# A two-expert-layer attention kernel: routing arithmetic of the second layer partly on GpSimd, its tables in three pieces, its first tile inside the attention's last step

## The chip, the cores and the metric

The kernel runs on one core of a Trainium2 chip. The time is the device time of one launch in microseconds; for the kernel before, the median of three runs is given. Engines are called as the profile calls them: PE (TensorE), DVE (VectorE), ACT (ScalarE), POOL (GpSimd), SP (SyncE, which here only issues DMAs).

## The reference

```python
x = x + 0.5 * ffn(layernorm(x))      # top-1 of 8 experts, 128 -> 512 -> 128
x = x + attn(layernorm(x))           # 16 sequences of 256 tokens, 16 heads of 8
x = x + 0.5 * ffn(layernorm(x))      # the same experts again

def ffn(x, Wr, br, W1, b1, W2, b2):
    expert = argmax(x @ Wr.T + br, axis=-1)
    h = relu(einsum('td,efd->etf', x, W1) + b1[:, None, :])
    y = einsum('etf,edf->etd', h, W2) + b2[:, None, :]
    return y[expert, arange(tokens)]
```

x is 16 x 256 x 128 in fp32, that is 4096 rows, or 32 tiles of 128 rows. The attention has rotary embeddings and a normalisation of q and k by head.

## The kernel before, in words

**Three stages.** The first expert layer (`experts(0)`), the attention (64 steps of one head group of one sequence, `step(n)`, n from 0 to 63 and a few more that drain it) and the second expert layer (`experts(1)`). An expert layer sorts the rows by expert into 39 tiles of 128 slots (`S_TILES`; each tile holds rows of one expert). For tile t, `x_transpose(t)`, `up(t)` (L862) and `down(t)` (L878) run on PE, `scale`, `load`, half of `relu` and `output` on DVE, the other half of `relu` and the copy of the expert's weights into `Ws` (`w_copy`) on ACT.

**What each step n of the attention does.** ACT takes exponentials of 2 x 512 columns (`exps`, L1231), PE makes the scores (L981), the products with the values (L1005) and, six steps ahead, scores for the row maxima (L958), which DVE reduces (L1769, `maxima`). For each sequence DVE multiplies the rotated q and k by their inverse roots (Rn, L1752), and POOL splits Rn into parts (`split`, L705 and L712). Each engine has its own list of instructions, written by its own `step(n)`; tables at the head of the file (`..._AT`) say at which n a piece of other work stands in it.

**The routing of the second layer** goes on under the attention, in four lots of tiles, `ROUTE_LOTS` = 0 to 11, 12 to 19, 20 to 25, 26 to 31. For a lot: mean and variance (`lot_layernorm` on POOL or `layernorm` on DVE), the inverse deviation (ACT, L1140 and L1142), logits (`lot_logits`), the one-hot choice (`one_hot`, `pick`), a running count over the lot's tiles (`lot_seen`: 8 scans, one for each expert), the count over partitions (`rank` on PE, L825 to L827), read back by `lot_take`, the slot of each row (`lot_place`: two tensor ops, a reduction and a cast on DVE), and at last one indirect DMA a tile from POOL that writes 128 rows into the DRAM tensor `slots` (`place`, L623). Behind each such DMA POOL writes 352 columns of a tile that nobody reads (`pause`, L603). Lots 0 to 2 are done in the attention, lot 3 within the tiles of the second layer (`last_lot(t, place)` spreads its DVE work over tiles 7 to 13).

**The tables.** `full_table` works out from the counts of the first three lots which expert and which rows of `slots` the first 19 tiles (`FULL`) have. SP waits for it and for all stores of lots 0 to 2, and then fetches tile after tile from `slots` (L536). `last_lot` makes the table of the other 20 tiles. There is a ring of 15 buffers for fetched tiles (`R_X2`): tile t + 15 is fetched when tile t has been written out.

**The end.** POOL's loop over t issues `scatter(t)`, an indirect DMA that writes tile t's rows to `out` (L632) as soon as DVE's `output` has finished them, with a pause of 480 columns behind. Before t = 3 stands the norm of lot 3, before t = 4 its logits, and behind t = 8 (`STORES_BEHIND`) the six stores of lot 3.

```python
for t in range(S_TILES):
    if t == LAST["norm"]:
        lot_layernorm(N_LOT + 1 + LAST_LOT)
    if t == LAST["logits"]:
        lot_logits(LAST_LOT)
    scatter(t)
    if t == STORES_BEHIND:
        for j in range(*ROUTE_LOTS[LAST_LOT]):
            place(LAST_LOT, j)
```

`fill_const` issues matmuls whose result nobody reads: 5 in step 50 (`FILL_TURN`), 6 in step 58, 9 behind the last step of the attention (`FILL_END`).

Of the kernel before, what the change touches and what calls it, by code (L numbers as in the profile page):

```python
# [5 lines left out]
P = 128  # L6
# [37 lines left out]
for RAMP_X in (RAMP_PE, RAMP_ACT, RAMP_DVE):  # L44
# [20 lines left out]
POOL_NORM_AT = {32: 0, 45: 1}  # L65
POOL_LOGITS_AT = {35: 0, 48: 1}
NORM_AT = {56: 2}
INVERSE_AT = {34: 0, 47: 1, 57: 2}
LOGITS_AT = {57: 2}
HOT_AT = {37: 0, 49: 1, 57: 2}  # L70
PICK_AT = {38: 0, 50: 1, 57: 2}
SEEN_AT = {38: 0, 50: 1, 57: 2}
RANK_AT = {41: 0, 53: 1, 59: 2}
PLACE_AT = {42: 0, 54: 1, 59: 2}
STORE_AT = {43 + j: (j,) for j in range(12)} | {55: (12, 13), 56: (14, 15), 57: (16,), 58: (17, 18), 59: (19,),
                                                60: (20, 21), 61: (22, 23), 62: (24, 25)}
TABLE_AT = 60
# [5 lines left out]
STORES_BEHIND = 8  # L83
LATE_LOADS = 3
DRAIN_FIRST = {1: (65,)}
DRAIN_SECOND = {2: (66, 67), 3: (68,)}
# [7 lines left out]
def program(nc, x, wqkvT, wpT, g_rms, wrT, br, w1T, b1, w2T, b2,  # L94
# [14 lines left out]
    with ctx:  # L109
# [52 lines left out]
        Hot, Seen = (e_major[:].rearrange("p e j -> p j e") for e_major in (HotE, SeenE))  # L162
# [24 lines left out]
        Done = sb("Done", [P, N_EXP + 1])  # L187
        Run = sb("Run", [P, len(ROUTE_LOTS), N_EXP], BF16)
# [87 lines left out]
        lot_ready = sem("lot_ready")  # L276
        lg_terms = sem("lg_terms")
# [63 lines left out]
        END = N_ALL + 5  # L341
        LOT = [None, slice(0, 2), slice(2, CH)] + [slice(CH * c, CH * c + CH) for c in range(1, N_CHUNK)]
# [123 lines left out]
        def _(sp):  # L466
# [83 lines left out]
            sp.wait_ge(offs_ready, 2)  # L550
# [12 lines left out]
        def _(pool):  # L563
# [1454 lines left out]
```

## Time and profile before

| | |
|---|---|
| median of 3 runs | 482.1 us (481.16 to 483.43) |
| the profiled execution | 479.99 us |
| its span | 478.2 us |
| PE busy | 427.5 us (89%) |
| DVE busy | 382.0 us (80%) |
| ACT busy | 349.1 us (73%) |
| POOL busy | 349.1 us (73%) |
| granted TensorE clock, mean | 0.99 |

The span runs from the first to the last instruction; the time of the execution is 1.8 us longer. Busy shares are means over stages that have different limits, so the stage in question has to be looked at by itself. A timeline row has the start in us from the start of the span, the busy time in us, engine, line and operation, out<-in, the count of merged instructions, and in brackets how long the engine had been idle before and who ended that.

### The profile page before, as it was taken

To read this page: it belongs to the slowest core of one execution; us is meant where nothing else is said; L and a number is where in the kernel's file an instruction comes from. 1 tells how busy PE (TensorE), PEld (TensorE's weight loads), DVE (VectorE), ACT (ScalarE), POOL (GpSimd) and SP (SyncE) were. 2 spreads that over 40 slices of the span, in tenths; PEclk is the share of its full clock that TensorE was granted. 3 is DMA by queue.
4 is the path that set the end of the run, shared out by engine and by line. 5 is a ranking of instruction groups with operands and counts; after the bars stand their busy time and mean duration, and the time that the engine had idled before them with its cause. 6 is when DMAs were issued, how large, how long until landed. Compare 5 with 4: busy or idle time off the path is not lost.

```text
span 478.2 us, 14075 instructions
## 1 busy us (share of the span) xinstructions
PE 427.5 (89%) x4140; PEld 318.0 (66%) x4140; DVE 382.0 (80%) x1055; ACT 349.1 (73%) x782; POOL 349.1 (73%) x561
## 2 busy tenths in 40 slices
PE   7999999989878898999989998998888979899993
PEld 4347999767764565665656665565455559789993
DVE  4786788897888788988889889988888557687772
ACT  4416776777747998989989898888677947467771
POOL 8019898978857988698683974399766807798995
PEclk9899999999999999999999999999999999899998
DMA  7872434251100000000000000000011123223310
GB/s 205 252 290 57 95 86 152 64 178 42 29 25 18 14 15 14 13 8 14 10 14 2 3 3 3 2 13 14 21 36 37 36 54 80 74 71 96 77 33 13
DMA packets 28651, 27.03 MB, mean 57 GB/s; under 512 B 5685, under 2 KB 25948, under 8 KB 28019
## 3 DMA queue, kind: packets, MB, share of 16 engines
q1 hardware_dynamic: 24034, 17.65, 12.4%
q0 software_dynamic: 4544, 8.49, 6.6%
q8 instruction: 37, 0.61, 0.5%
q14 instruction: 36, 0.29, 0.2%
HBM read 16.56 MB, written 12.71 MB: 61 GB/s over the span
## 4 chain that ended last, share of the span: by engine, by line
PE 41%; DVE 23%; issue 12%; POOL 12%; ACT 7%; DMA 2%; DVEq 1%; ACTq 0%; POOLq 0%
DVE Smax L1769 8%; PE PS L862 8%; PE PS L878 8%; PE PS L1005 5%; PE PS L958 5%; PE PS L981 4%; POOL out L632 3%; PE PS L940 3%; POOL Unread L603 2%; DVE St L1388 2%; DMA Pt<-rows,TokI 2%; ACT Pt L1231 2%; PE PS L924 2%; PE PS L917 1%; PE PS L1035 1%
## 5 line engine op out<-in xcount | busy, mean ns | idle before, releaser
L1769 DVE TENSOR_REDUCE Smax<-PS 128x4 f32<-128x1024 f32 x128 | 155.8, 1224 | 30.8 <-PE PS L958 30.0
L1231 ACT ACTIVATE Pt<-PS 128x1024 f32<-128x1024 f32 x128 | 126.4, 1024 | 18.4 <-PE PS L981 15.1
L878 PE MATMUL PS<-W,HsT 128*128 x624 | 85.2, 280 | 3.7 <-DVE Ys L1640 3.6
L862 PE MATMUL PS<-XsT,Ws 128*128 128x128 f32 x624 | 84.0, 278 | 1.0 <-ACT XsT L1135 0.7
L878 PEld LDWEIGHTS PS<-W,HsT 128*128 128x128 f32 x624 | 76.8, 194 | 6.7 <-issue 5.7
L862 PEld LDWEIGHTS PS<-XsT,Ws 128*128 128x128 f32 x624 | 77.3, 194 | 4.5 <-ACT XsT L1135 1.9
L1005 PE MATMUL PS<-Pt,Vg 128*32 128x256 f32 x1024 | 68.5, 385 | 0.4
L705 POOL TENSOR_TENSOR HL<-Rn,Zero 128x512 fp32r<-128x512 f32 x28 | 35.3, 1283 | 38.1 <-DVE Rn L1752 36.6
L610 POOL DMA_INDIRECT Pt<-rows,TokI x39 | 40.3, 1034 | 29.9 <-DVE TokI L1586 19.4
L603 POOL MEMSET Unread<- 128x352 f32 (+1 forms) x140 | 62.0, 443 | 0.2
L958 PE MATMUL PS<-QkT 24*128 24x256 f32 x512 | 59.7, 306 | 2.0 <-DVE Smax L1769 1.7
L958 PEld LDWEIGHTS PS<-QkT 24*128 24x128 f32 x512 | 39.9, 184 | 28.1 <-ACT Pt L1231 22.8
L1629 DVE TENSOR_SCALAR HsT<-PS,Bs 128x128 f32<-128x128 f32 x144 | 43.8, 347 | 18.1 <-PE PS L862 17.0
L1135 ACT ACTIVATE Ws<-W 128x512 f32 x78 | 49.0, 631 | 10.9 <-DVE ExpI L1593 6.7
L1176 ACT ACTIVATE HsT<-PS,Bs 128x128 f32<-128x128 f32 x168 | 51.6, 367 | 5.1 <-PE PS L862 4.4
L632 POOL DMA_INDIRECT out<-AtCol x39 | 38.4, 985 | 20.7 <-DVE AtCol L1640 15.2
L1135 ACT ACTIVATE XsT<-PS 128x128 f32<-128x128 f32 x78 | 21.7, 279 | 43.2 <-PE PS L851 42.4
L981 PE MATMUL PS<-QkT 25*128 25x256 f32 x512 | 34.2, 325 | 18.7 <-DVE Smax L1769 9.9
L1135 ACT ACTIVATE QkT<-PS 128x512 fp32r<-128x512 f32 x64 | 38.4, 600 | 15.3 <-PE PS L940 14.4
L940 PE MATMUL PS<-I,HL 128*128 128x128 f32 x256 | 41.5, 285 | 6.0 <-DVE Smax L1769 3.6
L981 PEld LDWEIGHTS PS<-QkT 25*128 25x128 f32 x512 | 22.1, 183 | 33.2 <-issue 31.2
L623 POOL DMA_INDIRECT slots<-XX,SlotI x32 | 31.6, 986 | 14.5 <-ACT Pt L1231 10.0
(255 smaller groups left out, 725.2 us busy)
## 6 DMA issues: line engine op xcount, KB each, us to landing
AtCol<-slots SPq DMA_DIRECT2D x39, 65.5 KB, 1.9
rows<-XX SPq DMA_DIRECT2D x8, 288.0 KB, 4.3
XX<-x SPq DMA_DIRECT2D x8, 256.0 KB, 4.2
W<-w1T SPq DMA_DIRECT2D x2, 1024.0 KB, 6.2
W<-w2T SPq DMA_DIRECT2D x2, 1024.0 KB, 9.1
mid<-mid_second SPq DMA_DIRECT2D x1, 1472.0 KB
mid<-Ys SPq DMA_DIRECT2D x16, 64.0 KB
QkT<-NmaxT SPq DMA_DIRECT2D x64, 4.0 KB
```

The source lines that it names most:

```text
L603: nc.gpsimd.memset(Unread[:, 0:columns], 0.0).then_inc(paused, 1)
L632: pool.indirect_dma_start(out, bass.IndirectOffsetOnAxis(ap=Xs2[:, t % R_X2, P + 2:P + 3].bitcast(I32), axis=0), Xs2[:, t % R_X2, 0:P], No ...
L862: last = nc.tensor.matmul(PS[:, h_bank(n) + c // 2, (c % 2) * P:(c % 2 + 1) * P], Ws[:, n % R_WS, c * P:(c + 1) * P], XsT[:, n % 2, :], st ...
L878: last = nc.tensor.matmul(PS[:, y_bank(n), 0:P], HsT[:, n % 2, c, :], W2[:, ds(e * D_FF + c * P, P)], start=(c == 0), stop=(c == FC - 1))
L940: last = nc.tensor.transpose(PS[:, qkT_bank(m), qk * T + tt * P:qk * T + (tt + 1) * P], v, I[:])
L958: last = nc.tensor.matmul(PS[:, max_bank(m, pair) + h % 2, tt * T:(tt + 1) * T], QkT[rows, m % R_QK, 0, tt * P:(tt + 1) * P], QkT[rows, m ...
L981: last = nc.tensor.matmul(PS[:, score_bank(m, h // 2) + h % 2, c * T:(c + 1) * T], QkT[rows, m % R_QK, 1, c * P:(c + 1) * P], QkT[rows, m ...
L1005: last = nc.tensor.matmul(PS[32 * h:32 * h + 32, 6, 0:T], weights[:, c, at:at + 32], Pt[:, m % 2, h, c, :], start=(m % 2 == 0 and c == 0), ...
L1135: return nc.scalar.activation(dst, src, ACT.Copy)
L1176: last = nc.scalar.activation(HsT[:, n % 2, c, :], PS[:, h_bank(n) + c // 2, (c % 2) * P:(c % 2 + 1) * P], ACT.Relu, bias=Bs[:, n % 2, c:c ...
L1231: nc.scalar.activation(Pt[:, m % 2, 2 * pair:2 * pair + 2, :, :].rearrange("p h c t -> p (h c t)"), PS[:, score_bank(m, pair):score_bank(m ...
L1769: nc.vector.tensor_reduce(Smax[:, b % 2, :, at:at + 33:32].rearrange("p t h -> p h t"), PS[:, max_bank(m, pair):max_bank(m, pair) + 2, :]. ...
```

## The change

Lot work moves between engines and between steps:

- DVE's 8 scans a lot become one scan over all experts (`seen`, with a mask `FreshLot` of ones and zeros); the one-hot choice of a lot is cut into `lot_largest`, `lot_ties` and `lot_pick` in different steps.
- The slot arithmetic (`lot_place`) leaves DVE. POOL's new `lot_slots` does it in six dependent instructions.
- Norm and logits of lot 2 go from DVE to POOL.
- The stores of lots 0 to 2 stand later (`STORE_AT`: from step 48 to 64, where it was 43 to 62); for lot 2 the `rank` on PE moves from step 59 to 61.
- The expert table is made in three pieces: 13 tiles (`FIRST_FULL`) from lots 0 and 1, six more from lot 2 (`more_tiles`, `more_table`), 20 with lot 3. SP fetches the first 13 tiles when lots 0 and 1 are stored.
- The second layer begins in PE's step 64 (`begin`, `first`): tile 0 is transposed and multiplied before the last product with the values. DVE's `begin` stands in step 62; POOL copies the first three tiles' expert weights in step 60 (`first_weights`).
- The 5 filling matmuls of step 50 and the 9 at the end are gone, as is the `drain` of POOL between its attention steps and its loop over t.
- In that loop, norm and logits of lot 3 stand before t = 0, and `lot_slots` and the stores of lot 3 behind t = 4. DVE starts on lot 3 at t = 6 instead of 7.

```diff
-POOL_NORM_AT = {32: 0, 45: 1}
-POOL_LOGITS_AT = {35: 0, 48: 1}
-NORM_AT = {56: 2}
-RANK_AT = {41: 0, 53: 1, 59: 2}
+POOL_NORM_AT = {32: 0, 44: 1, 57: 2}
+POOL_LOGITS_AT = {35: 0, 46: 1, 59: 2}
+LARGEST_AT = {38: 0, 50: 1, 59: 2}
+SEEN_AT = {46: 0, 54: 1, 60: 2}
+RANK_AT = {47: 0, 55: 1, 61: 2}
+POOL_SLOT_AT = {47: 0, 55: 1, 61: 2}
+WEIGHTS_AT = 60
+TABLE_AT, SCALE_AT, MORE_AT = 58, 62, 63
-STORES_BEHIND = 8
+STORES_BEHIND = 4
-FILL_TURN, FILL_MAXIMA, FILL_END = {50: 5}, {58: 6}, 9
-LAST = {"norm": 3, "inverse": 6, "logits": 4, "rank": 9}
+FILL_MAXIMA = {58: 6}
+LAST = {"norm": 0, "inverse": 5, "rank": 9}
...
+            def over_experts(into, values, r, op):
+
+                lot_link(nc.gpsimd.tensor_tensor(Half[:, r], values[:, r, 0:4], values[:, r, 4:8], op))
+                lot_link(nc.gpsimd.tensor_tensor(Half[:, r, 0:2], Half[:, r, 0:2], Half[:, r, 2:4], op))
+                lot_link(nc.gpsimd.tensor_tensor(into[:, r], Half[:, r, 0], Half[:, r, 1], op))
+
+            def lot_slots(i):
+                r = LOT_ROWS[i]
+                shape = [P, r.stop - r.start, N_EXP]
+                pool.wait_ge(*emptied("rank", i))
+                lot_link(nc.gpsimd.tensor_tensor(Place[:, r], by_tile(SeenE, r), Base[:].unsqueeze(1).to_broadcast(shape), ALU.add))
+                lot_link(nc.gpsimd.tensor_tensor(Place[:, r], Place[:, r], by_tile(HotE, r), ALU.mult))
+                over_experts(SlotF, Place, r, ALU.add)
+                nc.gpsimd.tensor_copy(SlotI[:, r], SlotF[:, r]).then_inc(lot_ready, 1)
+
+            def first_weights():
+                pool.wait_ge(slots_ready, 2)
+                for t in range(R_WS):
+                    e = pool.value_load(tile_expert(1, t), min_val=0, max_val=N_EXP - 1)
+                    nc.gpsimd.tensor_copy(Ws[:, (S_TILES + t) % R_WS, :], W1[:, ds(e * D_FF, D_FF)]).then_inc(ws_ready, 1)
...
-            nc.gpsimd.drain()
             for t in range(S_TILES):
                 if t == LAST["norm"]:
                     lot_layernorm(N_LOT + 1 + LAST_LOT)
-                if t == LAST["logits"]:
                     lot_logits(LAST_LOT)
                 scatter(t)
                 if t == STORES_BEHIND:
+                    lot_slots(LAST_LOT)
                     for j in range(*ROUTE_LOTS[LAST_LOT]):
                         place(LAST_LOT, j)
...
+                if n == TAIL - 1:
+                    pe.wait_ge(exp_ready, 2 * n - 1)
+                    begin()
                 if n < 0 or not group(n + QKT_LEAD):
                     small(n)
+                if n == TAIL - 1:
+                    first()
...
-                for e in range(N_EXP):
-                    last = nc.vector.tensor_tensor_scan(Seen[:, r, e], OneCol[:, r], Hot[:, r, e], 0.0, ALU.mult, ALU.add)
-                return last
+                return nc.vector.tensor_tensor_scan(flat(SeenE, r), FreshLot[:, N_EXP * r.start:N_EXP * r.stop], flat(HotE, r), 0.0, ALU.mult, ALU.add)
...
+            def lot_largest(i):
+                r = LOT_ROWS[i]
+                dve.wait_ge(lg_ready, i + 1)
+                mark(nc.vector.tensor_reduce(Mx[:, r], Lg[:, r], AX, ALU.max))
+                settled()
+                mark(tt_(by_tile(HotE, r), Lg[:, r], over_experts(Mx, r), ALU.is_ge))
```

**The order on POOL, steps 55 to 61, after the change.** The engine that stores the rows; the six rows with Place, Half and SlotF are `lot_slots` of lot 1, those with Dm, Mean and Var the norm of lot 2, those with XX and Lg its logits, and "COPY Ws" a weight copy.

```order
L772 CAST SlotI<-SlotF 128x8
L647 DMA slots<-XX,SlotI 33920x131
L627 MEMSET Unread 128x352
L647 DMA slots<-XX,SlotI 33920x131
L627 MEMSET Unread 128x352
L647 DMA slots<-XX,SlotI 33920x131
L627 MEMSET Unread 128x352
L682 TENSOR_TENSOR Dm<-St 128x6
```

Three stores (tiles 11 to 13) stand between the slots of lot 1 and the norm of lot 2. The same engine, from the norm's last instruction to the logits of lot 2:

```order
L692 TENSOR_TENSOR Var<-Var,Dm 128x6
L647 DMA slots<-XX,SlotI 33920x131
L627 MEMSET Unread 128x352
L647 DMA slots<-XX,SlotI 33920x131
L627 MEMSET Unread 128x352
L647 DMA slots<-XX,SlotI 33920x131
L627 MEMSET Unread 128x352
L647 DMA slots<-XX,SlotI 33920x131
L627 MEMSET Unread 128x352
L744 TENSOR_TENSOR XX<-Mean,XX 128x6
L746 TENSOR_TENSOR Lg<-Lg,XX 128x48
```

Four more stores (tiles 14 to 17) stand between that norm and the logits. Before, POOL had nothing but stores at this place; the slots of lot 1 and the norm and logits of lot 2 were DVE's.

**The order on PE, steps 60 to 65.** L1005 and L1065 are products with the values, L981 and L1041 scores, L825 to L827 and L881 to L883 the rank of lot 2, L862 and L918 `up`. As it was, from step 59:

```order
L825 MATMUL PS<-Run,Ones 128x8
L826 MATMUL PS<-SeenE,Ahead 128x8
L827 MATMUL PS<-Run,Ones 128x8
L1025 MATMUL PS<-I,Yn 128x128 x2
L1005 MATMUL PS<-Pt,Vg 32x256 x8
L981 MATMUL PS<-QkT 128x256 x8
L1035 MATMUL PS<-Wp,YnT 128x136 x2
L1005 MATMUL PS<-Pt,Vg 32x256 x8
L981 MATMUL PS<-QkT 128x256 x8
L1015 MATMUL PS<-I,YuT 128x128 x4
```

The rank stood ahead of the turn of Yn (L1025). The same engine as it is now, from step 60:

```order
L1095 MATMUL PS<-Wp,YnT 128x136 x2
L1065 MATMUL PS<-Pt,Vg 32x256 x8
L1041 MATMUL PS<-QkT 128x256 x8
L881 MATMUL PS<-Run,Ones 128x8
L882 MATMUL PS<-SeenE,Ahead 128x8
L883 MATMUL PS<-Run,Ones 128x8
L1075 MATMUL PS<-I,YuT 128x128 x4
L1065 MATMUL PS<-Pt,Vg 32x256 x8
L1041 MATMUL PS<-QkT 128x256 x8
```

The rank, which waits for DVE's count of lot 2, stands two steps later, right before the turn of the last but one sequence's outputs (L1015, now L1075).

**The order on POOL at the head of the second layer, after the change** (L656 is `scatter`):

```order
L744 TENSOR_TENSOR XX<-Mean,XX 128x6
L746 TENSOR_TENSOR Lg<-Lg,XX 128x48
L748 TENSOR_SCALAR XX<-XX 128x6
L749 TENSOR_TENSOR Lg<-Lg,Br 128x48
L656 DMA out<-AtCol 4096x128
L627 MEMSET Unread 128x480
L656 DMA out<-AtCol 4096x128
```

Before, three scatters stood ahead of the norm and one more ahead of the logits; now norm and logits stand ahead of all 39.

## Rows read from the trace of the kernel before

**Rows 1.** Timeline of POOL, from lot 3's stores to the end.

```profile
415.69 0.97 POOL L623 DMA_INDIRECT slots<-XX,SlotI  x1 [0.83 <-DVE SlotI L1913]
...
471.98 0.97 POOL L632 DMA_INDIRECT out<-AtCol  x1 [0.16 <-issue]
473.26 0.97 POOL L632 DMA_INDIRECT out<-AtCol  x1 [0.30 <-issue]
```

**Rows 2.** Timeline of all engines, from the attention's last exponential to tile 0.

```profile
381.16 1.02 ACT L1231 ACTIVATE Pt<-PS 128x1024 f32<-128x1024 f32 x1
381.26 0.97 POOL L623 DMA_INDIRECT slots<-XX,SlotI  x1 [0.17 <-issue]
...
385.42 13.88 SPq L536 DMA_DIRECT2D AtCol<-slots  x14
...
388.33 1.16 PE L862 MATMUL PS<-XsT,Ws 128*128 128x128 f32 x8 [0.37 <-ACT XsT L1135]
```

**Rows 3.** Timeline of PE, up(5), and the rank of lot 3.

```profile
399.24 1.06 PE L862 MATMUL PS<-XsT,Ws 128*128 128x128 f32 x8
...
410.14 0.17 PE L825 MATMUL PS<-Run,Ones 128*128 128x8 bf16 x1 [2.15 <-DVE Run L1895]
```

**Rows 4.** Busy time by stretch: us, PE, PEld, DVE, ACT, POOL, clock, DMA share, GB/s.

```profile
383.50:388.30 4.80, 2.36 (x12) 0.87 (x10) 0.78 (x4) 0.79 (x3) 0.00 (x0) 1.00 0.17 43
...
408.00:414.40 6.40, 4.26 (x24) 4.14 (x25) 3.83 (x27) 1.61 (x6) 4.72 (x8) 0.73 0.19 56
```

**Rows 5.** Timeline of POOL, steps 51 and 52: the split of sequence 15, stores.

```profile
341.31 2.52 POOL L705 TENSOR_TENSOR HL<-Rn,Zero 128x512 fp32r<-128x512 f32 x2 [1.85 <-DVE Rn L1752]
...
345.49 0.99 POOL L623 DMA_INDIRECT slots<-XX,SlotI  x1 [0.16 <-issue]
...
347.06 0.97 POOL L623 DMA_INDIRECT slots<-XX,SlotI  x1 [0.17 <-issue]
```

**Rows 6.** Timeline of DVE, step 50: lot 1's choice, scans, and Rn.

```profile
336.00 0.22 DVE L1429 TENSOR_REDUCE Mx<-Lg 128x8 f32<-128x64 f32 x1 [0.66 <-POOL Lg L725]
...
339.68 0.71 DVE L1443 TENSOR_TENSOR_SCAN SeenE<-OneCol,HotE 128x8 bf16<-128x8 f32 x8
...
340.54 0.69 DVE L1752 TENSOR_TENSOR Rn<-Rot,Rr 128x512 f32<-128x512 f32 x1
```

**Rows 7.** Timeline of POOL: norm of lot 1 (first, last), logits of lot 3.

```profile
321.63 0.22 POOL L658 TENSOR_TENSOR Dm<-St 128x8 f32<-128x8 f32 x1
...
323.32 0.20 POOL L668 TENSOR_TENSOR Var<-Var,Dm 128x8 f32<-128x8 f32 x1
...
404.27 0.28 POOL L722 TENSOR_TENSOR Lg<-Lg,XX 128x48 f32<-128x48 f32 x1
...
405.36 1.04 POOL L632 DMA_INDIRECT out<-AtCol  x1 [0.23 <-issue]
```

**Rows 8.** Timeline of DVE, steps 58 to 60: lot 2, a residual, the table.

```profile
367.97 0.20 DVE L1422 TENSOR_TENSOR Lg<-Lg,XX 128x48 f32<-128x48 f32 x1
...
370.48 0.17 DVE L1503 TENSOR_TENSOR Run<-Run,SeenE 128x8 bf16<-128x8 bf16 x1
...
373.92 0.42 DVE L1790 TENSOR_TENSOR XX<-PS,XX 128x256 f32<-128x256 f32 x1 [1.50 <-PE PS L1035]
...
379.28 0.16 DVE L1531 TENSOR_TENSOR Done<-End 128x7 f32<-128x7 f32 x1
```

**Rows 9.** Timeline of PE and of ACT: rank of lot 2, exponentials of steps 60 and 62.

```profile
370.80 0.17 PE L825 MATMUL PS<-Run,Ones 128*128 128x8 bf16 x1 [0.31 <-DVE Run L1503]
...
373.02 1.94 ACT L1231 ACTIVATE Pt<-PS 128x1024 f32<-128x1024 f32 x2 [0.35 <-PE PS L981]
...
377.59 1.94 ACT L1231 ACTIVATE Pt<-PS 128x1024 f32<-128x1024 f32 x2 [0.29 <-PE PS L981]
```

**Rows 10.** Timeline of ACT: the half of relu(5), the inverse of lot 3.

```profile
400.62 0.62 ACT L1176 ACTIVATE HsT<-PS,Bs 128x128 f32<-128x128 f32 x2
...
403.26 0.21 ACT L1142 ACTIVATE XX<-LnVar 128x6 f32<-128x6 f32 x1
```

More of the change, by code:

```diff
@@ L825, in rank @@
                     nc.tensor.matmul(PS[:, bank, 0:N_EXP], Ones[:], Run[:, i - 1, :], start=True, stop=False)
-                last = nc.tensor.matmul(PS[:, bank, 0:N_EXP], Ahead[:], Seen[:, ROUTE_LOTS[i][1] - 1, :], start=(i == 0), stop=True)
+                last = nc.tensor.matmul(PS[:, bank, 0:N_EXP], Ahead[:], lot_total(i), start=(i == 0), stop=True)
                 last = nc.tensor.matmul(PS[:, bank, N_EXP:2 * N_EXP], Ones[:], Run[:, i, :], start=True, stop=True)
@@ new lines, in begin, with first, run @@
+                def begin():
+                    pe.wait_ge(slots_ready, k + 1)
+                    x_transpose(0)
+                def first():
+                    up(0)
+                    x_transpose(1)
+                def run():
+                    for t in range(1 if k else 0, S_TILES + 1):
+                        if k and t - 1 in TABLES:
+                            pe.wait_ge(slots_ready, TABLES[t - 1])
+                        if t < S_TILES:
+                            up(t)
+                        if t >= 1:
+                            e = pe.value_load(tile_expert(k, t - 1), min_val=0, max_val=N_EXP - 1)
+                        if k and t == LAST["rank"]:
+                            rank(LAST_LOT)
+                        if not k and tail(t):
+                            max_scores(t - TAIL_TILE, 0)
+                        if k:
+                            for n in DRAIN.get(t, ()):
+                                step(n)
+                        if t + 1 < S_TILES:
+                            x_transpose(t + 1)
+                        if t >= 1:
+                            down(t - 1, e)
+                        if not k:
+                            if t == WP_TURN:
+                                wp_turn()
+                            if t == WP_ROUTER:
+                                wp_router()
+                            for n in RAMP_PE.get(t, ()):
+                                step(n)
@@ L915, in fill_const @@
+                return begin, first, run
             def fill_const(count, bank=7):
@@ L1195, in run @@
                     for t in range(S_TILES):
-                        if k:
-                            for n in DRAIN_FIRST.get(t, ()):
-                                step(n)
-                        first = not tail(K0 + t) and not (k and t in DRAIN_SECOND)
+                        first = not tail(K0 + t) and not (k and t in DRAIN)
                         if first and t + 1 < S_TILES:
@@ L1367, in _ @@
             begin, run = experts(1)
-            for n in range(RAMP_END, TAIL):
+            for n in range(RAMP_END, TAIL - 1):
                 step(n)
-                if n == TAIL - 2:
-                    begin()
             run()
@@ L1423, in scaled_logits, with ranks, over_experts, settled @@
                 link(tt_(Lg[:, r], Lg[:, r], Br[:].unsqueeze(1).to_broadcast(shape), ALU.add))
+            def ranks(r):
+                return Rank[:].unsqueeze(1).to_broadcast([P, r.stop - r.start, N_EXP])
+            def over_experts(values, r):
+                return values[:, r].unsqueeze(2).to_broadcast([P, r.stop - r.start, N_EXP])
+            def settled():
+                dve.wait_ge(step_done, links[0])
+            def mark(ins):
+                links[0] += 1
+                ins.then_inc(step_done, 1)
@@ L1688, in rope_tables @@
                 half = HD // 2
+                link(nc.vector.memset(FreshLot[:], 1.0))
+                for r in LOT_ROWS:
+                    nc.vector.memset(FreshLot[:, N_EXP * r.start:N_EXP * r.stop:r.stop - r.start], 0.0)
                 dve.wait_ge(rope_in, 16 * 5)
```

434 lines of the change are left out of this document (222 added, 212 removed).

## Prediction

> **What bounds the kernel now.** I read the end first. POOL's timeline shows that the last 36 indirect DMAs (six stores of lot 3, then the scatters of tiles 9 to 38) follow each other without a real gap: from 415.69 to the 35th at 471.98 are 34 times 1.655 us, and the last comes 1.28 us later, at 473.26, since it has no pause ahead [rows 1]. Where a wait would stand, "issue" stands with 0.16 to 0.30 us. So the end is set by POOL's queue; the span of 478.2 us ends 4.9 us behind the start of the last scatter. PE runs at 1.9 us a tile there, slower than POOL empties its queue, but POOL began late.
>
> Then the joint of attention and second layer. The last exponential ends at 382.18, POOL's last store of lot 2 starts at 381.26, SP sees it landed and fetches the first tiles at 385.42, and up(0) starts at 388.33 [rows 2]. A store is thus visible 4.2 us behind its start, and 2.9 us more pass until the first tile is on PE. up(5) is at 399.24, and before up(10) PE idles 2.15 us for the rank of lot 3 [rows 3]; in the stretch around that wait the granted clock is 0.73, so about half of it ran at 1.2 GHz [rows 4].
>
> **The change, by the path that sets the end.** A faster PE in the second layer buys nothing by itself; what counts is when POOL can start its unbroken queue. Now norm and logits of lot 3 stand ahead of scatter(0), and the logits wait for ACT's inverse behind relu(5). Call T0 the start of scatter(0). All 45 indirect DMAs and the new slot arithmetic follow it. So I work out T0 and then add the queue.
>
> *1. Split of sequence 15.* From here on POOL will be full. It starts at 341.31 now, when DVE has made Rn [rows 5]. In step 50 DVE spends 0.66 us waiting for POOL's logits, about 0.9 on the first three ops and 1.4 on pick and eight scans (0.71) before Rn at 340.54 [rows 6]. The change leaves there two ops of about 0.25 each, so 2.4 us of DVE's time go; part was cover for the maxima's matmuls, and I count 1.9. From lot 0, seven scans and the slot arithmetic (1.2 us) leave DVE, spread over steps 38 to 43; about half of DVE's time there showed up in the steps, so 0.9. The split starts at 338.5. Bounds: 341.3 (nothing gained) and 337.6.
>
> *2. POOL's queue in the attention.* Split to first store 4.2 us, then 1.57 us from this store to the next [rows 5]. Behind the split now come 16 stores (tiles 2 to 17, at 1.55: 24.8), lot_slots(1), the norm of lot 2 and its logits. The norm took 1.9 us (321.63 to 323.52) and with its joint 2.1; the logits with their four instructions 1.2 [rows 7]. lot_slots is six dependent instructions on POOL, which no row shows; its nearest are POOL's small tensor ops, 0.20 to 0.28 us and a hand-over of 0.08: 2.1 us with the joint to the next DMA. Bounds 1.7 and 3.0. Sum 24.8 + 4.2 + 2.1 + 2.1 + 1.2 = 34.4, and the logits of lot 2 are ready at 338.5 + 34.4 = **372.9**. Before, DVE had multiplied them at 367.97 [rows 8].
> On 48 columns the multiplication of the logits takes POOL 0.28 us [rows 7] and DVE 0.20 [rows 8], a ratio of 1.4. The Trainium skill, "GPSIMD Engine Reference", section "Performance versus the Vector engine", puts ordinary elementwise work at about 2x (1.96 for its add) and so speaks against this move; the trace disagrees at this size. By the page's ratio, lot_slots would be an estimated 2.6 us instead of 2.1, and the end 1.0 us later (two lots on the path). I take the rows'.
>
> *3. DVE and PE, steps 59 to 61.* The 13-tile table (4.3 us, from there to 379.44 [rows 8]) stands in step 58 and is done at about 369, ahead of the logits: free. From 372.9 follow choice, scan and running count of lot 2 (367.97 to 370.65 are 2.7 us; less 0.4 for two logits ops and 0.5 for seven scans: 1.8), between them the residual with its statistics (1.0, from 373.92 to the table), then PE's rank: 372.9 + 2.8 + 0.2 = **375.9**. It was at 370.80 and two steps earlier [rows 9]. The exponentials of step 62 need rank, turn, values and scores behind it: 370.80 to 373.02 for the same kind of list, 2.5 with the longer turn. So they start at 378.4, not 377.59 [rows 9]: the attention ends at 382.18 + 0.8 = 383.0 although its steps 38 to 57 were some 3 us faster. All that is saved before is lost in this wait.
> *The clock.* PE reaches the rank at about 370.2 and waits 5.7 us. A wait of 2.15 us brought the granted clock of a stretch to 0.73 [rows 3, 4]: 6.4 us with 27% missing, which is 3.4 us at half speed, 1.7 us of work. I take 1.5 us here; bounds 0 and 3.0. The attention ends at 384.5.
>
> *4. Tile 0.* up(0) follows at once, with 0.4 us for the copy of the transposed tile: **384.9**, 3.4 us earlier than 388.33. The data are there: store 19 starts at 372.9 + 0.2 + 1.6 = 374.7, landed 4.2 later, on PE 2.9 later at 381.8 [rows 2]. POOL's three weight copies are ready by 381 and cost nothing on this path.
>
> *5. up(0) to T0.* up(0) to up(5) takes 10.9 us now; values(63) comes in between (1.0), and DVE's eight small table ops in tiles 1 to 5 (some 1.6 us busy, a third of it felt, 0.5): 12.4. From up(5) to the end of relu(5) on ACT 2.0; inverse 0.5; logits 1.1; joint 0.3 [rows 3, 7, 10]: 3.9. T0 = 384.9 + 16.3 = **401.2**. POOL itself is free by then: two stores, three copies (1 to 1.7 us each), slots, six stores and the norm end near 395.
>
> *6. The queue.* 44 x 1.655 to the last scatter, less 0.37 for the missing pause, plus lot_slots(3) 2.2: 74.6. Last scatter at 475.8, against 473.26 [rows 1]. **+2.5 us.** The rank of lot 3 is no stall any more (its scan is done at t = 7), about 4 us on PE, but PE is not what ends last. For the same reason the later fetches may wait (tile 19 for lot 3's stores, tile 20 for the ring) without cost: PE would end near 471. The drain before the loop cost nothing: POOL had its stores out and no tile to scatter yet. The five and nine filling matmuls lay in waits; their removal is in items 1 and 4, and a clock that falls without them is in the bound of the clock.
>
> The profiled execution took 479.99 us, so the sum gives 482.5; that execution was 2.1 us below the median shown, and I add the difference to the median: 482.1 + 2.5 = **484.6 us**.
>
> **The rivals.** 0.5% is 2.4 us, about what a measurement of this kernel tells from no change. My sum lies at that edge.
> - *A, POOL's queue makes PE wait at step 61 and the clock falls* (forecast): 483.5 to 488, mostly just above +2.4 us. For it: the count of stores between slots(1) and the logits, which is in the order, not a guess. Chance 0.55; of it 0.40 over the edge.
> - *B, the same wait, but no loss of clock, or a shorter queue*: item 3 without the clock gives +1.0, 483.1 us; with lot_slots at its low bound (two lots) 482.3. For it: at the joint before, PE was busy 2.36 of 4.8 us and the clock stayed at 1.00 [rows 4]. Against: the wait now is as long by itself and nothing fills it. Chance 0.22, nearly all within the edge.
> - *C, faster.* If the logits of lot 2 came in time (split at 337.6, DVE slack in steps 51 to 57 used up by nothing), the attention would end at 382.2 - 0.9 - 1.9 - 1.2 (norm of lot 2 off DVE ahead of the last maxima) = 378.2. Then tile 0's data decide. It would need POOL's logits by 369.0, 4 us earlier than I find; store 19 starts then at 370.8, up(0) at 378.6 at best, T0 at 394.9 and the last scatter at 469.5: -3.8, 478.3 us. It decides if POOL's queue from the split takes under 31 us instead of 34.4. Against: 24.8 of them are counted DMAs. Chance 0.18.
> - *D, the second layer starves PE so long that POOL runs dry*, by the late landing of lot 3's stores and half clock: tile 19 on PE at T0 + 18.7 + 4.2 + 2.9 = T0 + 25.8, 20 more tiles 37.9, plus 3 for their waits and 3.5 for the clock, 70.2: still 4 us under the queue's 74.6. At twice those waits and that clock the end would be some 3 us later than A, 487.5. Chance 0.05.
>
> **How the numbers follow.** Forecast 484.6. Slower by over 0.5%: 0.40 from A, 0.05 from D. Within: 0.15 from A, 0.20 from B, 0.01 from C, so 0.36. Faster: 0.17 from C and 0.02 from B, 0.19. The range: below it reaches into C (479.0), above it takes in the clock's high bound, slots at 3.0 and a split that gains nothing, not all at once: 488.0.
>
> **What would show it.** In the profile after: the split at 338 to 339 and POOL unbroken from there to its copies; DVE's Mx of lot 2 released by POOL's Lg near 373; PE idle 5 to 6 us ahead of L881, with a granted clock below 1 behind; up(0) near 385; scatter(0) near 401, released by POOL's own logits, and then 1.65 us a DMA to the end. I am wrong if PE does not wait at the rank of lot 2, if scatter(0) starts before 398, or if the last scatters are released by DVE (then PE sets the end).

## The result and the profile after

The changed kernel takes 485.66 us (median of 17 runs, 483.99 to 487.09), the kernel before 481.44 us beside it (median of 17, 479.71 to 484.75). The ratio is 1.0081 with a 95% interval of 1.0061 to 1.0101: slower by about 4 us. The profiled execution took 485.71 us with a span of 483.9 us. The one of before took 479.99 us with a span of 478.2 us and lay 1.45 us below its median here; so the two profiles differ by 5.7 us where the medians differ by 4.2.

The forecast was 484.6 us, by +2.5 us in POOL's queue of scatters. The time came out 1.1 us from it, but what makes it up is something else, so that the number is close is luck.

First the end of POOL's timeline in the changed kernel, which answers to [rows 1]; columns as there (start, us, engine, line, operation, idle time ahead and what released it).

```profile
461.09 0.97 POOL L656 DMA_INDIRECT out<-AtCol  x1 [0.17 <-issue]
462.06 0.52 POOL L627 MEMSET Unread<- 128x480 f32 x1
462.74 0.97 POOL L656 DMA_INDIRECT out<-AtCol  x1 [0.17 <-issue]
...
473.96 0.97 POOL L656 DMA_INDIRECT out<-AtCol  x1 [0.31 <-issue]
```

The scatters follow each other in 1.65 us without a gap, as before, and the last starts at 473.96, only 0.7 us later than before (473.26). But the span does not end 4.9 us behind that start any more: it ends 9.9 us behind it. What fills this stretch is not in the timeline at all. It is in the list of the instructions that close the program, by engine (count, duration in ns as smallest/median/largest, first and last start in us). In the kernel before it reads:

```profile
L109 ACTq DRAIN  x1: 654/654/654, 468.9 to 468.9; - x1
...
L109 DVEq DRAIN  x1: 330/330/330, 470.9 to 470.9; - x1
L109 POOLq DRAIN  x1: 6164/6164/6164, 471.8 to 471.8; - x1
```

And in the changed kernel:

```profile
L111 ACTq DRAIN  x1: 654/654/654, 462.0 to 462.0; - x1
...
L111 DVEq DRAIN  x1: 330/330/330, 464.0 to 464.0; - x1
L111 POOLq DRAIN  x1: 11391/11391/11391, 472.3 to 472.3; - x1
...
L111 SPq DRAIN  x1: 7/7/7, 476.3 to 476.3; - x1
```

The program closes with a drain on each engine, an instruction that in every trace here ends behind all work of its engine ahead of it. POOL's begins, in the records, while its last work is still under way, so its duration is not its price. From the end of the last scatter (473.96 + 0.97 = 474.94) to the end of the drain (472.3 + 11.39 = 483.68) it is 8.74 us. Before it was 3.74 us (474.23 to 477.97). That is 5.0 of the 5.7 us. The other 0.7 are POOL's queue.

The joint of attention and second layer, first on POOL and then on PE, answers to [rows 2, 5, 8, 9]:

```profile
338.25 2.53 POOL L729 TENSOR_TENSOR HL<-Rn,Zero 128x512 fp32r<-128x512 f32 x2 [1.45 <-DVE Rn L1878]
...
372.44 0.28 POOL L749 TENSOR_TENSOR Lg<-Lg,Br 128x48 f32<-128x48 f32 x1
...
374.58 0.97 POOL L647 DMA_INDIRECT slots<-XX,SlotI  x1 [0.17 <-issue]
...
394.54 0.20 POOL L682 TENSOR_TENSOR Dm<-St 128x6 f32<-128x6 f32 x1 [5.11 <-DVE St L1452]
...
398.60 1.07 POOL L656 DMA_INDIRECT out<-AtCol  x1 [0.25 <-issue]
```

```profile
375.50 0.17 PE L881 MATMUL PS<-Run,Ones 128*128 128x8 bf16 x1 [4.40 <-DVE Run L1579]
...
383.61 1.16 PE L918 MATMUL PS<-XsT,Ws 128*128 128x128 f32 x8
```

The split of sequence 15 starts at 338.25, POOL then has its unbroken list, the logits of lot 2 come at 372.7, and PE waits 4.40 us ahead of the rank. At 394.54 POOL has idled 5.11 us for DVE's statistics of lot 3. The granted clock behind that wait, from the table by stretches (length, busy us and count of PE, PEld, DVE, ACT, POOL, then the clock as a share of 2.4 GHz, DMA share, GB/s):

```profile
370.00:374.00 4.00, 1.10 (x22) 0.44 (x12) 1.04 (x6) 2.59 (x4) 3.52 (x9) 1.00 0.10 34
374.00:378.00 4.00, 2.50 (x23) 1.16 (x23) 2.40 (x11) 0.00 (x0) 3.75 (x8) 0.74 0.12 38
378.00:382.00 4.00, 3.58 (x42) 1.90 (x42) 0.99 (x4) 2.94 (x4) 2.66 (x8) 0.83 0.24 65
```

A quarter and a sixth of the clock are missing in two stretches of 4 us: together 3.4 us at 1.2 GHz. Still PE does its last matmul at 463.97, where it was 470.90 before. PE has become 7 us earlier, and nothing of it reaches the end.

### The profile page after: what moved, and what is told of

Read it like the earlier page. It is cut to its first block, busy times and chain, and to the rows that moved or that the text cites. A ratio compares the mean times of both kernels' runs of the same rounds, so it can differ in the third digit from the quotient of the medians.

```text
span 483.9 us, 14057 instructions
## 1 busy us (share of the span) xinstructions
PE 424.0 (88%) x4126; PEld 316.0 (65%) x4126; DVE 376.8 (78%) x1025; ACT 347.3 (72%) x779; POOL 359.6 (74%) x600
## 4 chain that ended last, share of the span: by engine, by line
PE 55%; DVE 18%; issue 10%; ACT 7%; POOL 5%; DMA 2%; DVEq 1%; ACTq 0%; POOLq 0%; SPq 0%
PE PS L918 11%; PE PS L934 11%; DVE Smax L1895 9%; PE PS L1065 8%; PE PS L1018 6%; PE PS L1041 6%; PE PS L1000 3%; ACT Pt L1297 3%; PE PS L984 3%; DVE St L1452 2%; PE PS L977 2%; PE PS L1095 2%; PE PS L907 2%; POOL Unread L627 1%; POOL out L656 1%
## 5 line engine op out<-in xcount | busy, mean ns | idle before, releaser
L918 PE MATMUL PS<-XsT,Ws 128*128 128x128 f32 x624 | 83.3, 276 | 0.7 <-ACT XsT L1200 0.4
L918 PEld LDWEIGHTS PS<-XsT,Ws 128*128 128x128 f32 x624 | 76.4, 192 | 4.5 <-ACT XsT L1200 1.4
L1065 PE MATMUL PS<-Pt,Vg 128*32 128x256 f32 x1024 | 69.6, 390 | 0.3
L634 POOL DMA_INDIRECT Pt<-rows,TokI x39 | 40.3, 1033 | 30.3 <-issue 25.2
L1200 ACT ACTIVATE Ws<-W 128x512 f32 x75 | 47.3, 631 | 11.1 <-DVE ExpI L1705 6.7
L1041 PE MATMUL PS<-QkT 25*128 25x256 f32 x512 | 34.8, 331 | 18.0 <-DVE Smax L1895 13.3
L1041 PEld LDWEIGHTS PS<-QkT 25*128 25x128 f32 x512 | 22.3, 186 | 33.1 <-issue 30.4
L656 POOL DMA_INDIRECT out<-AtCol x39 | 38.2, 979 | 6.8 <-issue 5.8
L1065 PEld LDWEIGHTS PS<-Pt,Vg 128*32 128x32 f32 x1024 | 26.9, 110 | 21.1 <-issue 1.7
```

The costliest lines, as they stand in the source:

```text
L918: last = nc.tensor.matmul(PS[:, h_bank(n) + c // 2, (c % 2) * P:(c % 2 + 1) * P], Ws[:, n % R_WS, c * P:(c + 1) * P], XsT[:, n % 2, :], st ...
L1041: last = nc.tensor.matmul(PS[:, score_bank(m, h // 2) + h % 2, c * T:(c + 1) * T], QkT[rows, m % R_QK, 1, c * P:(c + 1) * P], QkT[rows, m ...
L1065: last = nc.tensor.matmul(PS[32 * h:32 * h + 32, 6, 0:T], weights[:, c, at:at + 32], Pt[:, m % 2, h, c, :], start=(m % 2 == 0 and c == 0), ...
L1200: return nc.scalar.activation(dst, src, ACT.Copy)
```

## The experiments

All times of a kernel are medians; ratios are to the kernel before, run beside it on the same chip, with a 95% interval.

### 1. The drain alone, out of the kernel before

```diff
             for n in range(RAMP_END, END):
                 step(n)
-            nc.gpsimd.drain()
             for t in range(S_TILES):
```

> The kernel before, without its one drain of GpSimd ahead of the scatters, nothing else. Theory P (a drain pays for each indirect DMA since the drain before it): in the two profiles at hand three drains end 2.94, 6.08 and 7.95 us behind the last packet of the indirect DMAs, with 45, 97 and 142 indirect DMAs since the drain before; a line of about 0.6 us + 0.052 us each. So the program's last drain grows from 2.9 to 8.0 us, the queue of scatters stays (scatter 0 at 393.5, last near 473.3), span 483.2: +5.0 us, ratio 1.010. Theory Q (the drain in the attention was free, and the long end of the changed kernel comes from its new work on POOL): last drain 2.9 us as before, ratio 1.000. Theory R (the end grows with all instructions of POOL since the last drain, 100 against 609 records: 0.0098 us each): the same +5 here, told apart by the other runs.

Measured: 486.43 us, ratio 1.0078 (1.0039 to 1.0117). The closing drain of POOL:

```profile
L109 POOLq DRAIN  x1: 11352/11352/11352, 473.6 to 473.6; - x1
```

It ends at 484.94, 8.74 us behind POOL's last work (476.20), to a hundredth as in the changed kernel, whose new work on POOL is not in this one. So theory Q falls, and the one deleted line costs, within the intervals, as much as the whole change (1.0081). The last scatter starts at 475.23 here and not at 473.3: this profile has stretches of half clock near 313 and 389 us that the one of before lacks, so of its 7.0 us of longer span 5.0 are the drain.

### 2. The drain put back into the changed kernel

```diff
             for n in range(RAMP_END, END):
                 step(n)
+            nc.gpsimd.drain()
             for t in range(S_TILES):
```

> The changed kernel with the drain put back where it was, between the last store of lot 2 and the norm of lot 3. Its last store starts at 388.05, last packet near 391.3, 97 indirect DMAs: by P and R the drain ends 6.1 us later, 397.4, the norm starts there and not at 394.54, so scatter 0 moves from 398.6 to about 401.5, the last scatter to 476.8, and behind it come 0.97 + 3.74 and not 0.97 + 8.75 us: span 481.7, -2.2 us against the change (ratio to before about 1.004). Theory Q (drain never mattered for the end): the end stays 8.75 us and scatter 0 is later, +2.9 us, ratio to before 1.015.

Measured: 483.26 us, ratio 1.0031 (1.0003 to 1.0059), span 480.8. The drain ended at 396.14, scatter 0 started at 400.41, and the closing drain ended 3.74 us behind the last scatter's end (476.83), as P says. It gives back about half of the loss (3.1 of the 5.7 us of span). Of the other 2.6, 1.9 are lost since this drain, with 97 indirect DMAs ahead of it, takes 8.03 us and delays the norm of lot 3 by 1.7 (396.24 instead of 394.54); 0.7 are the queue as in the changed kernel.

### 3. A drain where POOL idles

```diff
             def step(n):
+                if n in (30,):
+                    nc.gpsimd.drain()
                 if STATS_AT.get(n - 1, 0) >= POOL_LOTS:
```

> The changed kernel with one drain in step 30, ahead of split(10), where POOL idles 5.72 us for DVE's Rn and where the last indirect DMA is over 10 us old. 71 indirect DMAs before it, 71 behind it. P: this drain takes 0.6 + 71 x 0.052 = 4.3 us and lies in the idle time (no step longer), the last drain ends 4.3 us behind the last packet and not 7.95: span 480.2, -3.6 us against the change, ratio to before 1.000 to 1.001. R (by all instructions, 314 before it, 295 behind): last drain 4.9 us, span 480.8. Q: nothing gained, ratio 1.008. A fourth theory, S (the end is long because stores and scatters of the last 140 us come so close that GpSimd's queue of descriptors is still full, whatever was drained before): end 7.95 as in the change, ratio 1.008.

Measured: 483.18 us, ratio 1.0027 (1.0000 to 1.0054), span 481.9. The drain in step 30 and the closing one:

```profile
L782 POOLq DRAIN  x1: 6669/6669/6669, 257.0 to 257.0; - x1
L111 POOLq DRAIN  x1: 8832/8832/8832, 472.9 to 472.9; - x1
```

Both end 5.9 us behind the work ahead of them (257.74 to 263.64, 475.81 to 481.69), with 71 indirect DMAs each. The first comes 10 us after the last packet of any of them (247.6), so it does not wait for data to land, and P was wrong to count from the last packet: the drain ends 16.0 us behind that and 5.9 behind POOL's work. The 71 ahead of it are all gathers (L634 and L665 of this kernel, rows fetched into SBUF), the 71 ahead of the closing one all stores and scatters, so at this number the direction does not matter either. The closing drain is shorter by 2.9 us where my line said 3.6; theory S, by which the early drain would change nothing, falls. One step of the attention became 0.36 us longer (4.06 instead of 3.70), since 5.9 us are a little more than the idle time. The last scatter came 0.9 us later than in the changed kernel's profile (474.84); where the other 0.5 arose is open.

### 4. Six drains, for their length

```diff
+                if n in (10, 18, 26, 30, 34, 38):
+                    nc.gpsimd.drain()
```

> The changed kernel with six drains, in steps 10, 18, 26, 30, 34 and 38, each ahead of a split, for the length of a drain. Indirect DMAs since the drain before: 63, 4, 4, 0, 0, 0, and 71 at the end; other instructions of POOL: 154, 38, 38, 13, 29, 17, and 178. P: 3.9, 0.8, 0.8, 0.6, 0.6, 0.6 us, and 4.3 us behind the last packet at the end. R (0.0098 us for each record, of either kind, and about 2 us fixed): 4.1, 2.4, 2.4, 2.1, 2.3, 2.2 and 4.4. If all are the same length, the number does not matter and the line through three points was chance.

Measured (one execution, 483.39 us, span 481.6), the drains in steps 10, 18, 26, 30 and 34:

```profile
L782 POOLq DRAIN  x1: 7139/7139/7139, 184.6 to 184.6; - x1
L782 POOLq DRAIN  x1: 3319/3319/3319, 215.3 to 215.3; - x1
L782 POOLq DRAIN  x1: 3328/3328/3328, 245.6 to 245.6; - x1
L782 POOLq DRAIN  x1: 837/837/837, 257.6 to 257.6; - x1
L782 POOLq DRAIN  x1: 331/331/331, 276.2 to 276.2; - x1
```

In the kernel before, the drain that the change deletes, and the first scatter behind it on POOL's timeline:

```profile
L771 POOLq DRAIN  x1: 9522/9522/9522, 381.1 to 381.1; - x1
```

```profile
393.50 0.97 POOL L632 DMA_INDIRECT out<-AtCol  x1 [10.86 <-DVE AtCol L1640]
```

It ended at 390.66, 8.02 us behind POOL's work and 2.8 us before the first output was there: it lay in idle time.

All drains read as before, from the end of POOL's own work to the end of the drain (the count of other instructions is good to about 5):

| indirect DMAs since the last drain | other instructions of POOL | us | seen in |
|---|---|---|---|
| 0 | 13, 29, 17 | 0.08, 0.08, 0.07 | this kernel |
| 4 | 38 | 1.43, 1.44 | this kernel |
| 26 | 163 | 2.22 | the versions of 9 |
| 45 | 55, 61 | 3.74 | before, and 2 |
| 63 | 154 | 5.25 | this kernel |
| 71 | 243, 178 | 5.90, 5.88 | 3, this kernel |
| 97 | 366, 401 | 8.02, 8.03 | before, 2 |
| 142 | 467, 421 | 8.74, 8.74 | changed, 1 |

A drain behind 29 other instructions and no indirect DMA is free, and the price repeats to some hundredths at the same number of indirect DMAs: R falls. But P's straight line falls too: the price grows by about 0.08 us for each indirect DMA from 26 to 97, but lies above that line at 4 and by 3 us below it at 142 (0.7 us for the last 45). All six profiles that end with 142 show 8.74 us. Why it flattens is open, so the table should not be read beyond its rows.

### 5. Two scatters ahead of the norm of lot 3

```diff
-STORES_BEHIND = 4
+STORES_BEHIND = 6
-LAST = {"norm": 0, "inverse": 5, "rank": 9}
+LAST = {"norm": 2, "inverse": 5, "rank": 9}
```

> The changed kernel with scatters 0 and 1 ahead of the norm of lot 3 (which waits until 394.54 for DVE's statistics while POOL idles 5.1 us and the outputs of tiles 0 and 1 are there from 389.3 and 391.3), and lot 3's stores two scatters later in the list, so that all else keeps its place. Theory E1 (the end is POOL's queue of 1.655 us an indirect DMA, then the drain): scatter 0 at 389.5, every scatter from the third on two places, 3.3 us, earlier: last at 470.7, span 480.6, ratio to before 1.002 (the drain's 8.7 us behind the last scatter still in it). Theory E2 (PE, that ends at 464.0, or the data of tile 19 set the end): no change, 1.008.

Measured: 482.08 us, ratio 1.0011 (0.9980 to 1.0042), span 480.9. Scatter 0 started at 390.18 and the last at 470.96 (expected 470.7), PE's end did not move (464.05). Theory E1: the end is POOL's queue and the drain.

### 6. Shorter pauses

```diff
-LONG_PAUSE = 480
+LONG_PAUSE = 352
```

> The changed kernel with the pause behind the scatters and lot 3's stores of 352 columns instead of 480 (0.41 us instead of 0.51). E1: 44 times 0.10 us, last scatter at 469.6 instead of 473.96, span 479.5, ratio to before 0.999. PE's end at 464.0 is then still 5.6 us ahead. E2 (something else ends the program): no change. E3 (the shorter pause takes DVE's port more often and slows PE's tiles, whose outputs are made by DVE): PE's end moves from 464.0 to behind 467 and the last scatters wait for DVE; gain under 2 us.

Measured: 481.44 us, ratio 0.9983 (0.9954 to 1.0013), span 479.8; last scatter at 469.85 (expected 469.6). PE's end came at 465.34, 1.4 us later, but with a stretch of half clock at 425 that the changed kernel does not have. That is E1 again; E3 is not needed.

### 7. The logits of lot 2 ahead of two stores

```diff
-            56: (12, 13), 57: (14, 15), 58: (16, 17), 59: (18, 19),
+            56: (12, 13), 57: (14, 15), 59: (16, 17, 18, 19),
```

> The changed kernel with the stores of tiles 16 and 17 behind the logits of lot 2 instead of ahead of them (same four stores in the same order, store 19 where it was). By my prediction's item 2 (the logits come late because of the stores counted ahead of them): logits ready 3.1 us earlier (369.7 instead of 372.8), PE's rank at 372.4 instead of 375.5, its wait 1.3 us instead of 4.4 and no half clock behind it; exponentials of step 62 near 375.5 instead of 379.06. up(0) then waits for the data of store 19 (374.6 + 4.2 + 2.9 = 381.7) instead of 383.61, and scatter 0 and the end come 1.9 us earlier: span 482.0, ratio to before 1.004. If PE's wait was for something else, the rank stays at 375.5; if PE's wait does not matter for the end, span 483.9.

Measured: 484.87 us, ratio 1.0062 (1.0032 to 1.0092), span 483.5. PE:

```profile
371.68 0.17 PE L881 MATMUL PS<-Run,Ones 128*128 128x8 bf16 x1 [1.34 <-DVE Run L1579]
379.77 0.45 PE L907 MATMUL PS<-I,Xr 128*128 128x128 f32 x1 [2.00 <-DVE Xr L1720]
380.93 1.92 PE L918 MATMUL PS<-XsT,Ws 128*128 128x128 f32 x8
```

and its clock:

```profile
378.00:382.00 4.00, 2.23 (x11) 2.26 (x11) 1.69 (x6) 0.52 (x2) 2.81 (x6) 0.54 0.32 81
382.00:386.00 4.00, 4.00 (x30) 2.40 (x30) 3.36 (x15) 1.79 (x5) 3.51 (x7) 0.61 0.39 100
```

The rank came 3.8 us earlier, with 1.34 us of wait, and the clock stayed full there: item 2's chain from the stores to the rank is right. But PE then waited for the data of tile 0, and the clock fell at that wait, for 6.8 us (eight matmuls in 1.92 instead of 1.16 us). Scatter 0 came only 0.8 us earlier (397.81). A wait taken from one place was paid at the next, with half clock.

### 8. Filling matmuls in the wait

```diff
                 pe.wait_ge(*free("rank", i))
+                if i == LAST_LOT - 1:
+                    fill_const(18, bank)
                 pe.wait_ge(totals_ready, i + 2)
```

> The changed kernel with 18 filling matmuls of 512 columns (about 0.22 us each, 4.0 us) on PE right ahead of the rank of lot 2, in the 4.4 us that it waits there, into the rank's own bank. If the clock falls because of that wait (in the changed kernel half clock from 375.95 to 379.36, 3.41 us, values of step 61 1.94 instead of 1.07 us): granted clock stays at 1.00, step 61 to step 62 takes 1.5 us less, up(0) at 382.1, scatter 0 and the end 1.5 us earlier. If the clock falls for another reason (activity before the wait): half clock as before, no gain, or a loss of up to 0.4 us.

Measured: 484.19 us, ratio 1.0058 (1.0020 to 1.0095). The profile has half clock from 136 to 157, before anything that was changed, so its span (490.3) says nothing, and its steps do:

```profile
377.98 4.06 PE L979 MATMUL PS<-Col 128*128 128x512 bf16 x18
382.23 0.18 PE L883 MATMUL PS<-Run,Ones 128*128 128x8 bf16 x1 [0.19 <-DVE Run L1581]
```

No stretch behind it is below full clock, and from the exponentials of step 61 to those of step 62 it takes 6.51 instead of 7.93 us. So the fall of the clock came from the wait and cost 1.4 us there, by one profile of each; in the other profiles that have the wait the step took 7.80 to 8.22 us.

### 9. Together, and what bounds next

The drains of 2 and 3, the order of 5 and the pause of 6 in one kernel; then the same with pauses of 256 columns; then that pause alone in the kernel before; then the fills of 8 on top of the second.

> The changed kernel with what the runs so far singled out, together: scatters 0 and 1 ahead of the norm of lot 3, pauses of 352 columns, a drain in step 30 and one ahead of scatter 0. Drains measured so far, from the end of POOL's work ahead of them: 0.1 us with 0 indirect DMAs since the last drain, 1.4 with 4, 3.7 with 45, 5.3 with 63, 5.9 with 71, 8.0 with 97, 8.7 with 142. The one in step 30 (71) lies in 5.7 us of idle time, the one at the joint has 26 behind it, 2.7 us, and ends near 391.2, 1.0 us behind where scatter 0 stood without it. Last scatter 470.96 + 1.0 - 4.1 = 467.9, then 0.97 + 3.74 + 0.2: span 472.8, against about 478.2 before and 483.9 for the change, ratio to before 0.988. If the gains don't add (PE's end, 464.0 to 465.3, or the drain's length set by something else), span above 475.

> The same with pauses of 256 columns (0.33 us, another 0.08 off each). POOL's queue would be through at 464.4, ahead of PE's last output near 465.6: theory E1 says that PE is the bound now, last scatter near 466, released by DVE, span 470.9, ratio 0.984. E3: the denser descriptors of POOL slow DVE and with it PE's tiles; PE's end behind 467, gain over the one with 352 under 0.5 us or a loss.

> The kernel before, with pauses of 256 columns behind scatters and lot 3's stores, nothing else. If both bounds lie close together there (POOL's queue last at 473.26, PE's last output at 471.2), the pause gives back only what lies between them: last scatter about 471.4, released by DVE, span 476.3, ratio 0.996; what the changed kernel gains over this one with the same pauses (5 us by the expectation above) is then the worth of its earlier PE. If PE's waits in the stretch from 395 to 430 were for POOL, PE also ends earlier and the ratio falls to 0.985.

> The version with pauses of 256 columns, both drains and scatters 0 and 1 first, with the 18 filling matmuls on PE ahead of the rank of lot 2. In the run that had them in the changed kernel alone, step 61 to step 62 took 6.51 instead of 7.93 us and the values behind the rank ran at full clock, but that profile had 20 us of half clock elsewhere. Here PE's last output sets the end, not POOL's queue, so what PE gains should reach the end in full: step 61 to 62 6.4 instead of 7.80 us, no half clock at 375, last scatter 461.9 instead of 463.34, span 466.9 instead of 468.3, ratio to before 0.9725 (0.9755 without the fills). If the lower clock only comes later instead (for a wait behind it, as at tile 0 when the logits came first), span 468.3 and the same ratio.

| kernel | median us | ratio to before | scatter 0 | last scatter | PE's end | span |
|---|---|---|---|---|---|---|
| changed, pauses 352 | 472.88 | 0.9797 (0.9761 to 0.9832) | 391.68 | 466.15 | 462.82 | 471.1 |
| changed, pauses 256 | 470.94 | 0.9755 (0.9716 to 0.9794) | 391.83 | 463.34 | 461.57 | 468.3 |
| the same, with fills | 470.18 | 0.9744 (0.9702 to 0.9786) | 392.99 | 464.53 | 463.23 | 469.5 |
| before, pauses 256 | 479.64 | 0.9922 (0.9882 to 0.9963) | 396.04 | 474.30 | 473.01 | 479.3 |

The first gained 1.7 us of span more than expected: 1.0 of it because scatter 0's delay by the drain at the joint fell into the idle time ahead of the norm of lot 3 and so cost nothing; the other 0.7 are open. The second, near POOL's norm and at its end:

```profile
391.83 0.97 POOL L656 DMA_INDIRECT out<-AtCol  x1 [3.04 <-issue]
393.30 0.97 POOL L656 DMA_INDIRECT out<-AtCol  x1 [0.17 <-issue]
394.53 0.37 POOL L682 TENSOR_TENSOR Dm<-St 128x6 f32<-128x6 f32 x1
...
462.06 0.97 POOL L656 DMA_INDIRECT out<-AtCol  x1 [0.17 <-DVE AtCol L1755]
463.34 0.97 POOL L656 DMA_INDIRECT out<-AtCol  x1 [0.30 <-issue]
```

```profile
L830 POOLq DRAIN  x1: 3731/3731/3731, 387.3 to 387.3; - x1
L111 POOLq DRAIN  x1: 5574/5574/5574, 462.5 to 462.5; - x1
```

The norm of lot 3 had been waited for in 5.11 us of idle time; now a drain and two scatters lie there. The last scatter but one is released by DVE: POOL's queue and PE's last tile end together. In the kernel before, the same pauses bring the gaps of the queue into the open:

```profile
469.59 0.97 POOL L632 DMA_INDIRECT out<-AtCol  x1 [0.58 <-issue]
471.42 0.97 POOL L632 DMA_INDIRECT out<-AtCol  x1 [0.54 <-issue]
473.03 0.97 POOL L632 DMA_INDIRECT out<-AtCol  x1 [0.31 <-issue]
```

There PE is late, and POOL waits for each output of the last tiles (an unbroken queue shows 0.17 there). The pause alone gave 0.9922, less than the queue would by itself, and the 0.985 of a PE that ends earlier lies outside the interval. In part PE's late end is this profile's: it has half clock near 154 and 389 us, which the one of before lacks. The two kernels with pauses of 256 columns ran in one batch: 470.94 against 479.64 us. Both have 45 indirect DMAs ahead of the closing drain, so the 8.7 us are the rest of the change together with the order of 5 (the kernel before has its norm behind three scatters anyway); the two are not told apart. The change does make PE earlier; it only could not show.

The fills missed. The clock stayed full and step 61 took 6.54 instead of 7.80 us, but counted from the first exponential of the attention (145.67 against 144.35) the last scatter came at 318.86 us against 318.99. Counted the same way, up(0) came 1.4 us earlier, but by up(7) 0.4 us of that were left, and from up(19) on PE was 0.3 us behind. Two waits took part of it: 1.06 us ahead of up(7) for ACT's copy, where the version without fills waits 0.75, and 0.41 us at 422.96 for DVE's work on tile 19, where it has no wait in the records. POOL's queue, which starts behind the stores of lot 2 and the drain, began 0.2 us earlier and was as long as without fills: what PE gained lay beside it. My sentence that PE alone set the end there was wrong.

## Why the prediction was right in time and wrong in one step

- *Item 1, the split at 338.5*: 338.25. It is close partly by luck: this profile lost 1.3 us to half clock in step 2 (5.89 instead of 4.62 us), where the kernel before lost nothing. Without that the split would have stood near 337.0, below the bound of 337.6, and DVE's relief would have shown as some 4 us where 2.8 were said.
- *Item 2, logits at 372.9*: 372.72, and DVE's maximum at 372.82. lot_slots with its joint added 2.3 us to the spacing of two stores for lot 1 (2.1 said), the norm 2.2 (2.1), the logits 1.0 (1.2). The six ops of lot_slots alone ran from 356.19 to 358.14, 1.95 us. With its joint it took 2.3 us for lot 1 and 2.5 for lot 3, between the 2.1 and 2.2 that I took and the 2.6 worked out by the Trainium skill's ratio.
- *Item 3, rank at 375.9, loss of 1.5 us by the clock*: rank at 375.50, 3.4 us at 1.2 GHz, and by experiment 8 a price of 1.4 us. Experiment 7 shows that the stores ahead of the logits cause the wait. The attention ended at 383.38 and not at 384.5: the rank was 0.4 us earlier, from it to step 62 it took 3.6 us with the slow clock where I had 2.5 + 1.5, and the last exponentials 4.3 instead of 4.6.
- *Items 4 and 5*: up(0) at 383.61 (384.9 said), up(0) to up(5) 11.3 us (12.4), up(5) to scatter 0 3.7 (3.9): scatter 0 at 398.60 instead of 401.2, only 0.6 us above the 398 below which I had called myself wrong. Not in the sum was POOL's wait for DVE's statistics ahead of the norm: the norm ended at 396.66, just before relu(5) did on ACT (396.92), so it cost nothing here, and with 1.7 us more it did (experiment 2).
- *Item 6, the queue*: 75.4 us instead of 74.6 (lot_slots with its joint 2.5 us in place of 2.2, and indirect DMAs of 1.03 to 1.07 us at its start), last scatter at 473.96. Said was +2.5 us, it is +0.7. PE's end was placed near 471 and came at 463.97: the second layer ran almost without waits (1.68 us for tile 19), which by item 6 had no price and had none.
- *Rival D*: its sum at twice the waits and the clock is 70.2 + 6.5 = 76.7, 2.1 us over the queue's 74.6, so 486.7 us and not 487.5. Nothing hangs on it.
- *The step that failed* is the sentence "The drain before the loop cost nothing". It was true of its place and false of the program. I took the 4.9 us from the last scatter's start to the end of the span as a constant; 3.7 us of them are the closing drain of POOL, whose length depends on the indirect DMAs since the drain before. The deleted drain had paid for 97 of them in idle time; without it the closing one pays for all 142, +5.0 us, on the path. No rival had this.

So A's mechanism took place up to scatter 0 and cost 0.7 us where 2.5 were said, and the 4 us by which the kernel is slower are the drain. The forecast put its 2.5 us on a median before of 482.1; beside the changed kernel that median was 481.44 and the difference 4.2 us. That the two times lie 1.1 us apart is luck. By the medians, +4.2 less 5.0, the rest of the change made the kernel about 0.8 us faster, an estimate that the interval of the ratio (1 us either way) does not set apart from nothing; by the two profiles it made it 0.7 us slower.

## What to carry to other kernels

Look at what lies between the last work and the end of the span, engine by engine, before taking it for a constant: here the closing drain of GpSimd is as long as the indirect DMAs since the last drain make it, and a drain in idle time moves that cost off the path. An engine's faster work is worth what the next queue lets through, so remove the bound first (the order at the joint, the pauses) and then time the change: the same change that lost 4 us is part of a kernel 12 us faster than the one before. A wait that is taken from PE in one place can return at the next one, and with a lower clock behind it.

## What the runs showed of the hardware

- A drain on GpSimd takes, from the end of its work, 0.08 us with no indirect DMA since the last drain, 1.4 with 4, 3.7 with 45, 5.9 with 71, 8.0 with 97 and 8.7 with 142, even 10 us after the last packet, and for gathers as for stores. The Trainium skill, "VectorE: DVE Perf Modes", section "The DRAIN you can't avoid", says of the drains that the runtime puts at the start and end of a program that they take a constant of about 12 ns on all five engines. The drains of these traces are recorded at lines of the kernel, so they need not be those, and the figure must not be taken for them. The opening ones are near it on four engines (7 to 10 ns) and take 0.19 us on GpSimd. The closing ones are 7 ns on SP, but 330 on DVE, 654 on ACT, and 3.7 to 8.7 us behind the last work on GpSimd.
- In 5 of the 14 profiles, of both kernels, the clock fell to half for 3.4 us at about 154 us, in the same step 2 and with no PE wait over 0.9 us ahead of it since 142 us in the changed kernel's profile; it cost 1.3 us. The rows of the stretch, the kernel before (first) and the changed one:

```profile
150.00:158.00 8.00, 6.33 (x76) 3.84 (x76) 7.02 (x16) 6.53 (x17) 5.81 (x8) 1.00 0.07 19
```

```profile
150.00:158.00 8.00, 6.48 (x60) 4.09 (x62) 5.69 (x16) 5.37 (x14) 5.80 (x8) 0.79 0.07 18
```

  The kernel before with shorter pauses has it too (0.79), the changed kernel with the drain put back does not (1.00), so it does not come from the change. Why some executions have it stays open.
- The wait ahead of the rank of lot 2 brought 3.4 us of half clock in some profiles and 6.8 in others of the same instructions there; the steps differed by up to 0.4 us.
